# The frequency stage of a metaformer block in a new step: the spectral product is turned by VectorE in 32x32 blocks and not by way of memory

## The chip, the cores and the metric

The kernel runs on one core of a Trainium2 chip. A core has TensorE (matmuls), VectorE, ScalarE, GpSimd (POOL), SyncE (SP, which issues transfers here) and 16 DMA engines. The metric is the device time of one launch, in microseconds (us). A second source is one execution recorded by the hardware profiler.

## What is computed

Input x has 32 images of 64 channels with 56 x 56 = 3136 tokens, float32. A first half normalizes over channels, convolves with a binary 3x3 weight and adds residuals. Then the tokens t pass through a layer norm and a spectral unit, whose result is added to t. Cut to what matters here:

```python
Vf = rfft(phi, n=4096, axis=0)                    # 16 filters
Uf_p = rfft(u, n=4096, axis=1)                    # u: image, token, channel
U_plus = irfft(Vf[None, :, :, None] * Uf_p[:, :, None, :], n=4096, axis=1)[:, :sl]
out = einsum('btkd,k,kde->bte', U_plus, s, Mpp)   # and the same for U_minus, and a short AR term
```

In the kernel all filters and channel matrices are folded into one 64 x 64 complex matrix H(f) per frequency, so that the unit becomes: transform the tokens, multiply each frequency's image-by-channel matrix by H(f), transform back.

## The kernel before

There are three parts: a preparation, a first loop over 16 pairs of images (normalization, convolution, first step of the transform; writes z), the frequency stage (`mix_frequencies`, line 905), and `finish`, which makes the last step of the inverse and adds the residual. The change lies in the frequency stage alone.

The stage runs over 32 units (`NUNIT`) of 64 frequencies (`NF`). `two_by_two` writes the first two units out and loops over pairs of the others, one body for each parity (`slot`). Each engine has its own program; they meet by semaphores. For unit u:

- **p_v** (line 1058): one matmul makes the filter spectra, which VectorE copies to `v_mov` in two instructions (1150, 1153).
- **x** (1069), 4 chunks of 4 matmuls on the whole array: the forward step of the images. The copies to `xf` are four instructions a chunk.
- **h** (1078), 16 chunks of 8 float16 matmuls in two 64-column tiles: H of each frequency, saved to `hf`.
- **mix** (1090), 4 chunks of 16 matmuls in four 32-column tiles: the product. The rows of the result are images, its columns (real or imaginary, channel). It is saved to `y_sb`, stored to memory (`y_scratch`, line 964) and loaded back with frequencies as rows (`yt`, 969). This turns it.
- **inv** (1105), 16 matmuls in eight tiles of 32 rows by 64 columns: the inverse step, saved to `wf`. GpSimd stores it to `w_scratch` with eight DMAs (1020).

A chunk is one bank of PSUM: `ring` has seven banks of 512 float32 and p_v has the eighth. The order is the list `PLAN`: x 4, h 16, inv 4, mix 4, in all 28 chunks. Chunk p has bank p % 7, and is saved by ScalarE where p is even and by VectorE where it is odd. In every unit the inverse is that of unit u - 2 (`LAG_INV`), so that y has time to go out and come back. After unit 31 there are two rounds with only an inverse.

Each engine works strictly in the order of that list. TensorE waits before each chunk until the earlier chunk of the same bank is saved (`bank_free`, 1033). The inverse waits for all four of its banks at once, for `yt` and for its matrix. The first mix chunk waits until all h are saved. The saving engine waits until its chunk is ready (`chunk_ready`), and for the first inverse chunk also for `w_free`: `wf` is there once, and POOL gives it free when its stores of the unit before have landed.

SP's queue, in `body` (972): after x chunk 3 the load of z and `fwd` for unit u + 2; after the last mix copy the y store and the load of `inv`; a wait for the store; the two y loads. After unit 1 four early loads for `finish` (`load_x1`, 988; 1568 KB each) follow in the same queue.

## Time and profile before

| | us |
|---|---|
| median of three runs | 1436.41 |
| lowest, highest | 1433.49, 1443.66 |
| profiled execution, its own time | 1433.59 |
| its span | 1431.9 |
| TensorE busy | 1174.5 (82%) |
| VectorE busy | 954.0 (67%) |
| ScalarE busy | 798.9 (56%) |
| GpSimd busy | 498.9 (35%) |

The span is cut into 40 slices on the page, here of 35.8 us each. The frequency stage's steps begin at 628.69 us (slice 18) and its last copy starts at 1170.69 us; after 1182.29 `finish` has begun to load. Busy time of TensorE is pipelined and its ends are modelled, so where the length of a piece of work counts, the start of the next one is taken. PEld is the loading of weights, which overlaps. A timeline row with a count merges so many instructions; the idle time in brackets is what stood before the first, with what ended it. The profile's line 1197 is ScalarE's copy helper and 1213 VectorE's, so tile names tell the copies apart.

### The profile page before, as it was taken

Reading aid. Unit: us, or ns where it says so; the run is one execution under the profiler, and the core shown is the slowest. Engines: PE = TensorE matmul, PEld = TensorE weight load, DVE = VectorE, ACT = ScalarE, POOL = GpSimd, SP = SyncE. Lnnn points to the kernel's source line nnn. Section 1 sums busy time; section 2 is a strip of 40 time slices with the busy share of each in tenths; the row PEclk is TensorE's granted clock in tenths of the full one; section 3 lists DMA queues with packets and bytes.
Section 4 is the critical chain, followed back from the end, with each engine's and each line's share of the span. In section 5 each row is a group of like instructions: output and inputs, shape, how many; then the busy total and the mean of one; then the engine's idle time right before and its main releaser. Section 6 shows DMA issues by size and latency. Waiting matters only on the chain. (4 is left out here: it accounts for less than half of the span.)

```text
span 1431.9 us, 37537 instructions
## 1 busy us (share of the span) xinstructions
PE 1174.5 (82%) x15089; PEld 779.4 (54%) x15089; DVE 954.0 (67%) x1420; ACT 798.9 (56%) x1487; POOL 498.9 (35%) x440
## 2 busy tenths in 40 slices
PE   1899999999999977688698998999899926865667
PEld 1455555555555543147577777777777713433334
DVE  5288888888888888636477777677777713433334
ACT  1787788778887853335366666566656612322223
POOL 2146556666655567200122332232232230000000
PEclk9999999999999988669899999999999977988778
DMA  7024545554455448426899999899989969978873
GB/s 228 1 91 133 166 155 182 188 162 149 154 181 172 149 133 185 140 82 187 263 281 300 270 283 299 272 275 291 291 267 284 284 177 359 406 313 341 327 314 135
DMA packets 179624, 317.66 MB, mean 222 GB/s; under 512 B 14805, under 2 KB 154423, under 8 KB 162935
## 3 DMA queue, kind: packets, MB, share of 16 engines
q1 hardware_dynamic: 164966, 257.47, 56.6%
q0 software_dynamic: 14592, 59.26, 11.8%
q8 instruction: 47, 0.77, 0.2%
q14 instruction: 19, 0.16, 0.0%
HBM read 162.93 MB, written 153.76 MB: 221 GB/s over the span
## 5 line engine op out<-in xcount | busy, mean ns | idle before, releaser
L1020 POOL DMA_DIRECT2D w_scratch<-wf x256 | 151.2, 594 | 430.5 <-ACT y_sb L1197 391.5
L491 POOL TENSOR_TENSOR u_t<-u_t,root 98x1024 f32<-98x1024 f32 x62 | 118.0, 1935 | 169.2 <-DVE root L799 169.2
L535 PE MATMUL ring_norm<-x_all,center 128*128 128x448 f32 (+2 forms) x384 | 148.1, 511 | 24.9 <-PEq L211 15.7
L1402 ACT ACTIVATE out_sb<-p_turn 128x392 f32<-128x392 f32 x128 | 62.7, 498 | 189.6 <-PE p_turn L1358 177.7
L1346 PE MATMUL p_out<-w_in,last_masked 128*98 128x512 f32 x256 | 141.2, 636 | 23.8 <-DMA w_in<-w_scratch 23.8
L1078 PE MATMUL ring<-v_mov,m_sta 105*64 105x128 f16 x4096 | 147.2, 221 | 14.3 <-DVE xf L1213 11.6
L1213 DVE COPY hf<-ring 128x512 f32<-128x512 f32 x256 | 156.1, 682 | 1.0
L1197 ACT ACTIVATE hf<-ring 128x512 f32<-128x512 f32 x256 | 144.7, 597 | 4.9
L1391 DVE TENSOR_TENSOR x_in<-p_out,x_in 98x512 f32<-98x512 f32 x96 | 65.4, 690 | 123.1 <-DMA x_in<-x_scratch 68.3
L594 PE MATMUL ring_norm<-u_t,step_masked 98*128 98x512 f32 x256 | 126.7, 623 | 21.9 <-POOL u_t L491 21.9
L1078 PEld LDWEIGHTS ring<-v_mov,m_sta 105*64 105x64 f16 x4096 | 119.9, 110 | 40.2 <-DVE xf L1213 16.8
L1090 PE MATMUL ring<-hf,xf 128*32 128x128 f32 x4096 | 123.3, 278 | 19.1 <-ACT wf L1197 8.8
L1090 PEld LDWEIGHTS ring<-hf,xf 128*32 128x32 f32 x4096 | 113.0, 112 | 45.0 <-issue 30.6
L491 POOL TENSOR_TENSOR xc_t<-xc_t,root 98x1024 f32<-98x1024 f32 x64 | 119.7, 1900 | 50.7 <-DVE root L799 50.7
L1197 ACT ACTIVATE xf<-ring 64x256 f32<-64x256 f32 x256 | 98.5, 385 | 66.8 <-PE ring L1069 64.5
L1213 DVE COPY xf<-ring 64x256 f32<-64x256 f32 x256 | 108.2, 423 | 32.4 <-PE ring L1069 28.1
L1069 PE MATMUL ring<-fwd,z_in 128*128 128x128 f32 x1024 | 122.2, 279 | 0.0
L1069 PEld LDWEIGHTS ring<-fwd,z_in 128*128 128x128 f32 x1024 | 121.7, 196 | 0.1
L535 PEld LDWEIGHTS ring_norm<-x_all,center 128*128 128x128 f32 x384 | 66.6, 192 | 84.5 <-issue 44.9
L1358 PEld LDWEIGHTS p_turn<-ident,x_in 98*128 98x128 f32 x384 | 47.1, 153 | 120.1 <-DVE x_in L1391 67.5
L567 PE MATMUL p_conv<-signs_padded,conv_w 64*64 64x392 bf16 x2304 | 109.2, 330 | 0.2 <-DVE x_all L755 0.2
L624 ACT ACTIVATE xc_t<-ring_norm 98x512 f32<-98x512 f32 x128 | 78.7, 615 | 46.1 <-PE ring_norm L546 46.1
(132 smaller groups left out, 1923.1 us busy)
## 6 DMA issues: line engine op xcount, KB each, us to landing
z_in<-z_scratch SPq DMA_DIRECT2D x32, 1076.5 KB, 9.7
z_scratch<-z_sb SPq DMA_DIRECT2D x16, 2048.0 KB, 8.9
y_scratch<-y_sb SPq DMA_DIRECT2D x32, 1024.0 KB, 12.7
yt<-y_scratch SPq DMA_DIRECT2D x64, 512.0 KB, 6.2
w_scratch<-wf POOLq DMA_DIRECT2D x256, 128.0 KB, 7.6
w_in<-w_scratch SPq DMA_DIRECT2D x8, 4096.0 KB, 15.8
x_all<-in_x SPq DMA_DIRECT2D x16, 1568.0 KB, 7.6
x_scratch<-x_t SPq DMA_DIRECT2D x16, 1568.0 KB
```

The source lines that it names most:

```text
L491: return eng.tensor_tensor(v, v, r, ALU.mult)
L535: nc.tensor.matmul(bank_of("cen", q, c)[:, 0:WID * n], keep["center"][:, h, :], x_of(q)[:, WID * row:WID * row + WID * n], start=True, sto ...
L567: mm = nc.tensor.matmul(bank[CH * out:CH * out + CH, h, 0:CW], keep["conv_w"][CH * k:CH * k + CH, t, CH * k:CH * k + CH], pad[q % 2][CH * ...
L594: nc.tensor.matmul(bank_of("z", q, c), keep["step1"][:, c // 2, :], u_t[q % 2][:, c, :], start=True, stop=True).then_inc(z_ready, 1)
L624: nc.scalar.activation(xc_t[q % 2][:, c, :], bank, ACT.Copy).then_inc(xt_copied, 1)
L1020: nc.gpsimd.dma_start(w_units[u, h, s, c], wf[64 * c:64 * c + 64, 2 * h + s].rearrange("p (g n) -> p g n", n=256)).then_inc(w_stored, 16)
L1069: mm = nc.tensor.matmul(bank[:, 128 * j:128 * j + 128], z_in[slot][:, at:at + 2 * CH], fwd[slot][:, NF:3 * NF], start=True, stop=True)
L1078: mm = nc.tensor.matmul(bank[CH * n:CH * n + CH, 2 * NF * i:2 * NF * i + 2 * NF], m_sta[:, e, :], v_mov[:, NF * (1 - n):NF * (3 - n)], sta ...
L1090: mm = nc.tensor.matmul(bank[32 * j:32 * j + 32, 128 * i:128 * i + 128], xf[:, f, :], hf[:, f, :, :].rearrange("p r e -> p (r e)"), start= ...
L1197: return nc.scalar.activation(dst, src, ACT.Copy)
L1213: return nc.vector.tensor_copy(dst, src)
L1346: nc.tensor.matmul(p_out[0:NB, c % BANKS, :], keep["last"][:, ACH * c // MASKG, :], w_in[w_slot][:, ACH * c:ACH * c + ACH, 128 * slot:128 ...
```

## The change

A step now makes mix and inverse of unit u - 1 and x and h of unit u (`LAG` 1). The order is mix 0, x 0, mix 1, x 1, mix 2, x 2, mix 3, x 3; then four turns; then h 0 to 15; then the inverse. Banks come from a table: mix 3 to 6, x 0, 1, 2, 0, h and inverse as `BANKS` says. `xf` is there twice.

y doesn't go to memory. The four mix banks are read by VectorE with `transpose`, which turns each block of 32 x 32: rows (partitions) of a block become its columns. Four instructions (turn 0 to 3) take 16 channels each, from all four banks, 512 elements per partition, and write `yt` with channels innermost, so each instruction's elements lie 256 bytes apart in the order it writes them. The 32 columns of a block are the real and imaginary parts of 16 frequencies for one channel, its 32 rows the images; turned, frequencies are rows. The order in which mix takes the frequencies (`f`) and the rows of the constant `inv` are rearranged to match. ScalarE and VectorE don't copy y. A mix bank is free when turn 3 is done.

The inverse has 8 matmuls in four tiles of 64 x 64, one pass, with contiguous moving rows. It waits for turn 3 and for its banks 6, 1, 2 and 0.

Saving: x and inverse chunks alternate between ScalarE (even) and VectorE (odd). Of the h chunks VectorE saves 2, 5, 8, 11 and 14 and ScalarE the other eleven; before it was eight each. The y store and loads leave SP's queue, the tensor `y_scratch` goes, and after unit 31 there is one round with mix, turns and inverse.

```diff
-    inv = inv.transpose(0, 1, 4, 2, 3, 5).reshape(NUNIT, 2 * NALPHA, 128)
-    inv = np.concatenate([inv, inv], 1)
+    inv = inv.transpose(0, 1, 4, 2, 3, 5).reshape(NUNIT, 4, 16, 2, 2 * NA)
+    inv = inv.transpose(0, 1, 3, 2, 4).reshape(NUNIT, 128, 2 * NA)
...
-PLAN = [("x", 4), ("h", 16), ("inv", 4), ("mix", 4)]
-TAIL = ("inv",)
-LAG_INV = 2
+TAIL = ("mix", "turn", "inv")
+LAG = 1
 RING = 7
-
-
-def unit_chunks():
-
-    seen, out = {}, []
-    for stage, count in PLAN:
-        for _ in range(count):
-            k = seen.get(stage, 0)
-            seen[stage] = k + 1
-            out.append((stage, k, len(out)))
-    return out
+FIRST_MIX = 3
+
+H_ON_VECTOR = (2, 5, 8, 11, 14)
+
+BANKS = {"mix": (3, 4, 5, 6), "x": (0, 1, 2, 0), "h": (1, 2, 0, 1, 2, 0, 3, 4, 5, 6, 1, 2, 0, 3, 4, 5),
+         "inv": (6, 1, 2, 0)}
+
+
+def owner(stage, k):
+
+    if stage == "turn":
+        return 1
+    return int(k in H_ON_VECTOR) if stage == "h" else k % 2
+
+
+def step_chunks():
+
+    out = []
+    for k in range(4):
+        out += [("mix", k), ("x", k)]
+    out += [("turn", k) for k in range(4)]
+    out += [("h", k) for k in range(16)]
+    out += [("inv", k) for k in range(4)]
+    return [(stage, k, p) for p, (stage, k) in enumerate(out)]
...
-        inv = [sb(f"inv{i}", [128, 2, 2 * NA]) for i in range(2)]
-        xf = sb("xf", [128, NF, NIMG])
+        inv = [sb(f"inv{i}", [128, 2 * NA]) for i in range(2)]
+        xf = [sb(f"xf{i}", [128, NF, NIMG]) for i in range(2)]
         hf = sb("hf", [128, NF, 2, CH])
 
-        y_sb = [sb(f"y_sb{i}", [128, NF // 4, 2 * CH]) for i in range(2)]
-        yt = [sb(f"yt{i}", [128, NIMG // 2, 2, CH]) for i in range(2)]
+        yt = sb("yt", [128, NIMG, CH])
...
-            def store_y(slot):
-                sp.dma_start(d["y"][slot].rearrange("i p n -> p i n"), y_sb[slot][:]).then_inc(y_stored[slot], 16)
-
-            def load_y(slot):
-                for h in range(2):
-                    src = d["y"][slot].rearrange("i (j m) n -> (i j) m n", j=4)[:, 16 * h:16 * h + 16, :]
-                    sp.dma_start(yt[slot][64 * h:64 * h + 64].rearrange("p m r e -> p (m r e)"),
-                                 src.rearrange("f m n -> f (m n)")).then_inc(y_loaded[slot], 16)
+                sp.dma_start(inv[slot][:], d["c_inv"][u]).then_inc(inv_loaded[slot], 16)
 
             def body(u, slot, use):
 
+                sp.wait_ge(chunk_ready, chunks_until(u, pos["x", 3]))
+                after_wait(sp, sp_turn)
                 if not known(u, NUNIT - 2, NUNIT - 1):
-                    sp.wait_ge(chunk_ready, chunks_until(u, pos["x", 3]))
-                    after_wait(sp, sp_turn)
                     load(u + 2, slot)
-                for e in range(2):
-                    sp.wait_ge(saved[e], chunks_until(u, pos["mix", 3], e))
-                after_wait(sp, sp_turn)
-                store_y(slot)
                 if not known(u, 0, 1):
                     load_inv(u, slot)
-                sp.wait_ge(y_stored[slot], 16 * use)
-                after_wait(sp, sp_turn)
-                load_y(slot)
...
-                    pool.wait_ge(saved[e], chunks_until(u + LAG_INV, pos["inv", 3], e))
+                    pool.wait_ge(saved[e], chunks_until(u + LAG, pos["inv", 3], e))
...
+            stage, k, _ = chunks[at]
+            if stage == "mix":
+                stage, k, at = chunks[pos["turn", 3]]
+            eng.wait_ge(saved[owner(stage, k)], chunks_until(w, at, owner(stage, k)))
...
-                            all_saved(pe, u, pos["h", 15])
-                            if is_first(u):
+                            all_saved(pe, u - 1, pos["h", 15])
+                            if known(u, LAG):
                                 pe.wait_ge(reals_done, 3)
                         for i in range(4):
                             for j in range(4):
-                                f = 16 * k + 4 * i + j
-                                mm = nc.tensor.matmul(bank[32 * j:32 * j + 32, 128 * i:128 * i + 128], xf[:, f, :],
-                                                      hf[:, f, :, :].rearrange("p r e -> p (r e)"),
+                                f = 16 * j + 4 * k + i
+                                mm = nc.tensor.matmul(bank[32 * j:32 * j + 32, 128 * i:128 * i + 128],
+                                                      xf[1 - slot][:, f, :], hf[:, f, :, :].rearrange("p r e -> p (r e)"),
                                                       start=True, stop=True, tile_position=(0, 32 * j))
+                        mm.then_inc(chunk_ready, 1)
                     else:
 
                         if k:
                             continue
                         for at in range(4):
                             bank_free(pe, u, pos["inv", at])
-                        pe.wait_ge(y_loaded[slot], 32 * (use - 1))
-                        pe.wait_ge(inv_loaded[slot], 16 * (use - 1))
-                        for c in range(2):
-                            for r in range(2):
-                                for n in range(4):
-                                    rows = slice(32 * n, 32 * n + 32)
-                                    mm = nc.tensor.matmul(
-                                        ring[64 * c:64 * c + 64, pos["inv", n] % RING, :], inv[slot][rows, r, :],
-                                        yt[slot][rows, 8 * c:8 * c + 8, r, :], start=(r == 0), stop=(r == 1),
-                                        tile_position=(32 * n, 64 * c))
-                                    if c and r:
-                                        mm.then_inc(chunk_ready, 1)
-                    if stage != "inv":
-                        mm.then_inc(chunk_ready, 1)
+                        pe.wait_ge(saved[1], chunks_until(u, pos["turn", 3], 1))
+                        pe.wait_ge(inv_loaded[1 - slot], 16 * (use if slot else use - 1))
+                        after_wait(pe, pe_turn)
+                        for h in range(2):
+                            for c, row in ((0, 0), (1, 1), (1, 0), (0, 1)):
+                                images = slice(16 * h + 8 * c, 16 * h + 8 * c + 8)
+                                rows = slice(64 * row, 64 * row + 64)
+                                mm = nc.tensor.matmul(
+                                    bank_of("inv", 2 * h + row)[64 * c:64 * c + 64, :],
+                                    inv[1 - slot][rows, :], yt[rows, images, :],
+                                    start=True, stop=True, tile_position=(64 * row, 64 * c))
+                                if c != row:
+                                    mm.then_inc(chunk_ready, 1)
...
-                        eng.wait_ge(w_free, u - 1)
-                    if (stage, k) == ("mix", first_mix) and not known(u, 0, 1):
-                        eng.wait_ge(y_stored[slot], 16 * (use - 1))
...
-                    elif stage == "mix":
-                        copy(y_sb[slot][:, 4 * k:4 * k + 4, :].rearrange("p i n -> p (i n)"), bank
-                             ).then_inc(saved[which], 1)
+                    elif stage == "turn":
+                        e = slice(16 * k, 16 * k + 16)
+                        nc.vector.transpose(
+                            yt[:].rearrange("p i e -> p e i")[:, e], ring[:, FIRST_MIX:FIRST_MIX + 4, :]
+                            .rearrange("p b (i r e) -> p e r (b i)", r=2, e=CH)[:, e]).then_inc(saved[which], 1)
...
-            for u in (NUNIT, NUNIT + 1):
-                unit(u, u % 2, u // 2 + 1, False, True)
+            unit(NUNIT, NUNIT % 2, NUNIT // 2 + 1, False, True)
```

## Rows read from the trace of the kernel before

**Rows 1.** The page: busy time of the engines (us, share of the span, instructions).

```profile
PE 1174.5 (82%) x15089; PEld 779.4 (54%) x15089; DVE 954.0 (67%) x1420; ACT 798.9 (56%) x1487; POOL 498.9 (35%) x440
```

**Rows 2.** Windows, whole stage: us, busy time by engine, PEclk, DMA share, GB/s.

```profile
646.69:1134.11 487.42, 431.12 (x9632) 359.91 (x9628) 348.92 (x658) 292.59 (x598) 133.57 (x226) 0.99 0.91 276
```

**Rows 3.** Waits, 640 to 1140: who waited for whom, us, times, longest.

```profile
PE ring L1105 <- DVE hf L1213: 26.3, 29, 1.2
...
PE ring L1078 <- DVE xf L1213: 10.9, 30, 0.4
```

**Rows 4.** Timeline, one steady step: start, us, engine, line, out<-in, idle before.

```profile
899.93 3.73 PE L1069 MATMUL ring<-fwd,z_in 128*128 128x128 f32 x32
...
901.03 1.57 ACT L1197 ACTIVATE xf<-ring 64x256 f32<-64x256 f32 x4 [1.64 <-PE ring L1069]
...
901.92 3.52 DVE L1213 COPY xf<-ring 64x256 f32<-64x256 f32 x8 [0.79 <-PE ring L1069]
...
903.60 1.53 PE L1078 MATMUL ring<-v_mov,m_sta 105*64 105x128 f16 x48
904.41 4.65 ACT L1197 ACTIVATE hf<-ring 128x512 f32<-128x512 f32 x8
905.47 4.88 DVE L1213 COPY hf<-ring 128x512 f32<-128x512 f32 x8
...
905.49 3.15 PE L1078 MATMUL ring<-v_mov,m_sta 105*64 105x128 f16 x80 [0.36 <-DVE xf L1213]
...
909.58 2.01 PE L1105 MATMUL ring<-yt,inv 32*64 32x512 f32 x32 [0.93 <-DVE hf L1213]
...
911.51 3.70 PE L1090 MATMUL ring<-hf,xf 128*32 128x128 f32 x128
911.74 1.09 ACT L1197 ACTIVATE wf<-ring 128x512 f32<-128x512 f32 x2 [2.68 <-PE ring L1105]
911.80 1.29 DVE L1213 COPY wf<-ring 128x512 f32<-128x512 f32 x2 [1.45 <-PE ring L1105]
...
915.14 0.57 PE L1058 MATMUL p_v<-fwd,z_in 128*105 128x192 f32 x2
```

**Rows 5.** Timeline, the first two units of the stage.

```profile
628.69 0.97 PE L1058 MATMUL p_v<-fwd,z_in 128*105 128x192 f32 x2 [1.56 <-DVE m_sta L1242]
...
635.62 1.73 DVE L1213 COPY xf<-ring 64x256 f32<-64x256 f32 x4 [0.77 <-PE ring L1069]
...
642.36 0.19 DVE L1183 TENSOR_SCALAR hf<-hf 64x64 f32<-64x64 f32 x1
...
643.06 3.70 PE L1090 MATMUL ring<-hf,xf 128*32 128x128 f32 x128 [2.51 <-DVE hf L1187]
...
657.66 5.37 PE L1090 MATMUL ring<-hf,xf 128*32 128x128 f32 x128 [1.85 <-DVE hf L1213]
```

**Rows 6.** Timeline, the end of the stage.

```profile
1134.11 0.57 PE L1058 MATMUL p_v<-fwd,z_in 128*105 128x192 f32 x2
...
1166.84 3.69 PE L1105 MATMUL ring<-yt,inv 32*64 32x512 f32 x32 [13.12 <-DMA yt<-y_scratch]
...
1170.69 1.29 DVE L1213 COPY wf<-ring 128x512 f32<-128x512 f32 x2 [8.58 <-PE ring L1105]
```

**Rows 7.** The page: DMA issues (count, KB each, us to landing), the y store.

```profile
y_scratch<-y_sb SPq DMA_DIRECT2D x32, 1024.0 KB, 12.7
```

**Rows 8.** Groups by form, VectorE: busy us, mean ns, idle before.

```profile
L1213 DVE COPY y_sb<-ring 128x512 f32<-128x512 f32 x64 | 44.1, 691 | 56.7 <-PE ring L1090 56.7
```

**Rows 9.** Windows in the mix of unit 1: the granted clock.

```profile
658.00:660.00 2.00, 2.00 (x53) 2.00 (x48) 0.00 (x0) 0.60 (x1) 0.00 (x0) 0.59 0.95 229
```

**Rows 10.** Timeline, steps 2 and 3: early x1 load, first w store.

```profile
670.66 0.56 SPq L990 DMA_DIRECT2D x_all<-x_scratch  x1
...
677.23 5.04 POOL L1020 DMA_DIRECT2D w_scratch<-wf  x8 [81.68 <-ACT y_sb L1197]
...
708.92 1.08 ACT L1197 ACTIVATE wf<-ring 128x512 f32<-128x512 f32 x2 [14.19 <-POOLq L1024]
```

More of the change, by code:

```diff
@@ L888, in chunk_is_there @@
 def chunk_is_there(stage, u):
-    return (u >= LAG_INV) if stage in TAIL else (u < NUNIT)
+    return (u >= LAG) if stage in TAIL else (u < NUNIT)
 def chunks_until(u, p, engine=None):
-    plan = unit_chunks()
+    if engine is None:
+        mine = [(stage, at) for stage, k, at in step_chunks() if stage != "turn"]
+    else:
+        mine = [(stage, at) for stage, k, at in step_chunks() if stage != "mix" and owner(stage, k) == engine]
     if isinstance(u, int):
-        return sum(1 for w in range(u + 1) for stage, _, at in plan
-                   if chunk_is_there(stage, w) and (w < u or at <= p) and engine in (None, at % 2))
@@ L900, in chunks_until @@
-    per_unit = sum(1 for _, _, at in plan if engine in (None, at % 2))
-    missing = LAG_INV * sum(1 for stage, _, at in plan if stage in TAIL and engine in (None, at % 2))
-    return per_unit * u - missing + sum(1 for _, _, at in plan if at <= p and engine in (None, at % 2))
+        return sum(1 for w in range(u + 1) for stage, at in mine
+                   if chunk_is_there(stage, w) and (w < u or at <= p))
+    missing = LAG * sum(1 for stage, at in mine if stage in TAIL)
+    return len(mine) * u - missing + sum(1 for stage, at in mine if at <= p)
@@ L905, in mix_frequencies @@
 def mix_frequencies(nc, d, keep):
-    chunks = unit_chunks()
-    NCH = len(chunks)
-    assert NCH % RING == 0 and NCH % 2 == 0
+    chunks = step_chunks()
     pos = {(s, k): p for s, k, p in chunks}
@@ L1027, in _, with bank_of @@
             store(0)
-            with pool.Fori(1, NUNIT - LAG_INV) as u:
+            with pool.Fori(1, NUNIT - LAG) as u:
                 store(u)
-            for u in range(NUNIT - LAG_INV, NUNIT):
+            for u in range(NUNIT - LAG, NUNIT):
                 store(u)
+        def bank_of(stage, k):
+            return ring[:, BANKS[stage][k], :]
         def bank_free(eng, u, p):
+            stage, k, _ = chunks[p]
+            same = [at for other, n, at in chunks if other != "turn" and BANKS[other][n] == BANKS[stage][k]]
             if not isinstance(u, int):
-                w, at = (u, p - RING) if p >= RING else (u - 1, p - RING + NCH)
-                eng.wait_ge(saved[at % 2], chunks_until(w, at, at % 2))
-                return
-            before = [(w, at) for w in range(u + 1) for stage, _, at in chunks
-                      if chunk_is_there(stage, w) and at % RING == p % RING and (w < u or at < p)]
-            if before:
+                w, at = (u, max(at for at in same if at < p)) if min(same) < p else (u - 1, max(same))
+            else:
+                before = [(w, at) for w in range(u + 1) for at in same
+                          if chunk_is_there(chunks[at][0], w) and (w < u or at < p)]
+                if not before:
+                    return
                 w, at = before[-1]
-                eng.wait_ge(saved[at % 2], chunks_until(w, at, at % 2))
+            stage, k, _ = chunks[at]
+            if stage == "mix":
+                stage, k, at = chunks[pos["turn", 3]]
+            eng.wait_ge(saved[owner(stage, k)], chunks_until(w, at, owner(stage, k)))
         def all_saved(eng, u, p):
@@ L1060, in unit @@
                 for stage, k, p in chunks:
-                    if not (tail if stage in TAIL else head):
+                    if stage == "turn" or not (tail if stage in TAIL else head):
                         continue
@@ L1064, in unit @@
                         bank_free(pe, u, p)
-                    bank = ring[:, p % RING, :]
+                    bank = bank_of(stage, k) if stage != "inv" else None
                     if stage == "x":
@@ L1139, in saver @@
         def saver(eng, which, copy):
-            mine = [(stage, k) for stage, k, p in chunks if p % 2 == which]
+            mine = [(stage, k) for stage, k, p in chunks if stage != "mix" and owner(stage, k) == which]
             first_inv = min(k for stage, k in mine if stage == "inv")
-            first_mix = min(k for stage, k in mine if stage == "mix")
             last_h = max(k for stage, k in mine if stage == "h")
```

29 lines of the change are left out of this document (13 added, 16 removed).

## The prediction

> **What bounds the kernel now.** I read the page first (busy shares, slices, costliest groups), then the windows of the frequency stage, the timeline of one step, the waits, and last the two ends of the stage. The page has TensorE busy for most of the span [rows 1]. In the frequency stage it is busy 431 of 487 us at a mean granted clock of 0.99 [rows 2], against 349 us for VectorE and 293 for ScalarE. The DMA share of 0.91 looks like a rival bound, but among the waits of the stage none has a transfer releasing a matmul; the one case by a detour lies in its first steps [rows 10]. TensorE's regular idle spots are the inverse, which waits for the last h copies (26.3 us over 29 steps), and the seventh h chunk, whose bank waits for the last xf copy (10.9 us over 30) [rows 3]. So a steady step is a TensorE step with about 1.3 us of holes.
>
> The timeline gives its parts [rows 4]. x runs from 899.93 to 903.60, 3.67 us. Six h chunks (48 matmuls) take 1.53 us, 0.255 each where nothing holds them. After a wait, the other ten take 3.15 us, held by the copies. The inverse takes 1.93 us (909.58 to 911.51), the mix 3.63 (to 915.14), and the p_v matmul 0.41 (the rest of the 15.62 us step). Steps 0 to 31 start at 628.69 and 1134.11 [rows 5, 6], so the mean is 16.3 us. The steady one is 15.6, and the rest lies in the first steps.
>
> **What goes.** The y store and both y loads of each unit leave SP's queue: 2 MB a unit [rows 7] of some 4.3 (276 GB/s for 15.6 us). They are hidden in the steady steps, so there they are worth nothing; if that cover were gone each would cost its landing time, 12.7 us for the store. At the end they do show: unit 31's inverse starts at 1166.84 after 13.12 us of waiting for yt, and the last wf copy ends at 1170.69 + 1.29 = 1171.98 [rows 6]. Four y_sb copies a unit (about 1.28 us on VectorE, as two copies at 0.64, and as much on ScalarE) go too.
>
> **What comes, and where it stands.** VectorE gets four block turns a unit, each 512 elements per partition from PSUM, and keeps five h copies instead of eight; ScalarE gets eleven. Added up, neither becomes the bound. VectorE: v_mov 0.83, x 3.52, turns 2.6, h 5 x 0.61, inverse copies 1.29, together 11.3 us. ScalarE: 3.14 + 11 x 0.58 + 1.09 = 10.6 us. TensorE's own work is unchanged, about 14 us. The inverse has half the matmuls, but each drives twice the rows in four 64x64 tiles instead of eight 32x64 ones, so I leave it at 1.93. Judged by sums, the step should shrink.
>
> It doesn't, because of the order. VectorE works its list as written: x1, x3, four turns, then h2, h5 and so on. h2 lies in bank 0, and h5 in bank 0 too. TensorE issues in order, so h5, and all ten chunks and the inverse behind it, wait until VectorE has copied x3, made four turns and copied h2. Counted from the start of p_v:
>
> - p_v 0.41, x 3.67, mix 3.63 alternating; seven more changes between whole array and column tiles. These changes cost little in the trace (the inverse-to-mix passage is within 1.93), and I add 0.05 each: x3 ends at 8.06.
> - VectorE starts its copy 0.18 later (ScalarE's first xf copy, 901.03, against the first x chunk's end, 899.93 + 0.92) and needs 3.52 / 2 = 1.76 us [rows 4]: 10.00.
> - Four turns at 0.65: 12.60. h2's copy, 0.61: 13.21. h5 starts at 13.26.
> - h6 is ready at 13.77; ScalarE starts 0.18 later and makes five copies (h6, h7, h9, h10, h12) at 4.65 / 8 = 0.58 us: 16.85. Bank 0 holds h12 and is one of the inverse's.
> - TensorE ends h15 at 13.26 + 11 x 0.255 = 16.07, waits 0.8, and makes the inverse from 16.90 to 18.83.
>
> The next p_v stands there: a step of 18.8 us with 4.7 us of holes (1.5 before h2, 2.4 before h5, 0.8 before the inverse) against 15.6. What waits behind h5 on TensorE is the inverse, so wf, POOL's stores of w, and the next step's mix.
>
> **The turn's price.** No row shows one. The nearest are copies of 512 elements out of PSUM: 691 ns alone, 0.64 back to back for y_sb's or wf's plain order (two in 1.29), 0.61 for hf's [rows 4, 8]. Below, I bound it by an element rate without any start cost: the reduce-free slope between the 256-element xf copy (0.44 pitch) and the 512-element one (0.61) is 0.34 us per 512, so 0.34 is the floor. Above, I take twice the 0.61 of hf, 1.22, for a turn that is passed over twice. I take 0.65, since pattern and size are nearest to the copies. Each 0.1 us of a turn is 0.4 us of step and 12.4 us in all.
> The Trainium skill speaks both ways. "Vector Engine (DVE) Microarchitecture Reference", on the reshape front end, has the 32x32 turn sustain one element per cycle per lane. "Advanced Engine Details and Errata", Memory Cachelines, says that accesses that each fall on another SBUF line of 16 bytes pay a penalty. The turn writes 4 bytes every 256. By the first a turn costs about what a copy does, by the second more. No row of before writes in such steps, so it stands as a rival below.
>
> **TensorE's clock.** The mix of unit 0 took 3.70 us after 2.5 us of idling, but that of unit 1, after 1.85 us, took 5.37 [rows 5], at a clock of 0.59 from 658 to 660 [rows 9]. So a hole of the size that each new step has can cost 1.67 us, or nothing. I put that at one step in five, 0.3 us: 19.1 us a step. The Trainium skill's "TensorE: Matmul & The Clock Gate", on PSUM-queue cycling, tells of the same: short idles between groups of matmuls make the clock go up and down.
>
> **The ends of the stage.** Step 0 has no mix and no turns. ScalarE gets h0 and h1, waits for h2 (its bank needs the x3 copy, 637.35), then makes nine copies, to about 643.2; three small fixes of the first unit (0.70, as before) bring the first mix to 643.9, against 643.06 [rows 5]. There are then 31 steps to the mix of unit 31, which comes 0.4 earlier for want of a p_v: 643.9 + 31 x 19.1 - 0.4 = 1235.6. After it: mix 3.63, turns 0.16 + 2.6, inverse 1.98, copies 0.85, in all 9.2: 1244.8. Last, the early x1 loads: issued at 670.66, before the first store of w (677.23), they held the next wf copies until 708.92 [rows 10]. Now they are issued near 652 and should be through near 686, where the second unit's wf copy is due at 680.5: 6 us. The last wf copy ends at 1250.8, 78.8 later than before's 1171.98. What follows (POOL's stores, 12 us to the first w) is the same. Against the profiled execution's own 1433.59 us (span 1431.9, 1.7 around it): 1512. That execution is 3 us under the median of the three runs, within their spread.
>
> **Rivals.**
> *The clock falls in most steps* (0.17). For it: the hole before h5 follows another of 1.5 us with only 0.77 us of work between. Against: steady steps keep 1.00 with holes of 0.9. Then +1.7 a step instead of 0.3: 1512 + 31 x 1.4 = 1555, more if the inverse too is at half speed.
> *The turn costs twice a copy* (0.18): the Trainium skill's penalty, here 1.22 instead of 0.65, four times on the path: +2.3 a step, 1583.
> *Faster* (0.05): the one thing that decides is whether h5 waits behind the turns. If VectorE had h2 saved by the time TensorE asks, the step would be 8.06 + 16 x 0.255 + 0.8 + 1.93 = 14.9 and the kernel would end at 643.9 + 461.9 - 0.4 + 9.2 = 1114.6, 57 before now: 1376. The bound lies at a step of (1171.98 - 643.9 + 0.4 - 9.2 - 6) / 31 = 16.6, which needs turns of about 0.1 us. The list order speaks against it.
> *Near equal* (0.05, of which 0.03 within 1%): turns near the floor, 0.34, with cheap changes give 17.2 to 17.5 a step, still over 1%; only with a shorter h stage as well does it reach 1440.
>
> **Numbers.** My case (step 18.2 to 19.8) has 0.55 and gives 1478 to 1534, likeliest 1512. The range takes in the clock rival whole and most of the dear turn: 1475 to 1585. A per cent either way is what a measurement can tell. Faster 0.05, same 0.03, slower 0.92.
>
> **What would show it.** In the steady steps of the new profile: starts of p_v 18.5 to 19.5 us apart; before h2 and h5 TensorE idle about 1.5 and 2.4 us, released by VectorE; turns of 0.65 to 0.7 us standing between VectorE's x3 and h2 copies; ScalarE idle near 1.9 us before h6; DMA share down by nearly half with no gain. Wrong would be: turns of over 1 us, granted clocks under 0.95 in the stage, x and mix together longer than 7.7 us, or h5 released by anything but VectorE.

## The result, and the profile after

The changed kernel takes 1597.9 us (median of four runs, 1594.74 to 1598.76) against 1434.95 for the kernel before (four runs on the same chip): a ratio of 1.112, 95% interval 1.108 to 1.116. Slower was forecast, and by the mechanism forecast, but the time lies above the range (1475 to 1585). The profiled execution took 1598.08 us.

The page of the changed kernel, busy time of the engines (as [rows 1]):

```profile
PE 1260.8 (79%) x14577; PEld 830.8 (52%) x14577; DVE 980.6 (61%) x1388; ACT 813.4 (51%) x1519; POOL 498.9 (31%) x440
```

TensorE executes 512 matmuls fewer than before and is busy 86 us longer. The groups on the page (line, engine, operation, out<-in, count | busy, mean ns | idle before, releaser) show 48 us of it in h. This is the row of h in the kernel before:

```profile
L1078 PE MATMUL ring<-v_mov,m_sta 105*64 105x128 f16 x4096 | 147.2, 221 | 14.3 <-DVE xf L1213 11.6
```

And these are the rows of h and of the turns in the changed kernel; the price of a turn is far over that of the copy in [rows 8]:

```profile
L1081 PE MATMUL ring<-v_mov,m_sta 105*64 105x128 f16 x4096 | 195.1, 276 | 145.5 <-DVE hf L1214 105.5
...
L1176 DVE STREAM_TRANSPOSE yt<-ring 128x512 f32<-128x512 f32 x128 | 118.3, 1045 | 3.9 <-PE ring L1094 2.9
```

The waits of the changed kernel from 640 to 1300 us (as [rows 3]: who waited for whom, us, times, longest):

```profile
PE ring L1081 <- DVE hf L1214: 102.1, 31, 3.4
...
PE ring L1081 <- DVE xf L1214: 37.7, 30, 1.3
```

The first is h5's wait for its bank, the second h2's. These idle times of TensorE are called holes below. A steady step in the timeline of the changed kernel (as [rows 4]: start, us, engine, line, out<-in, idle before):

```profile
907.82 0.57 PE L1060 MATMUL p_v<-fwd,z_in 128*105 128x192 f32 x2
...
908.33 1.08 PE L1094 MATMUL ring<-hf,xf 128*32 128x128 f32 x32
...
909.34 1.16 PE L1071 MATMUL ring<-fwd,z_in 128*128 128x128 f32 x8
...
910.42 1.08 PE L1094 MATMUL ring<-hf,xf 128*32 128x128 f32 x32
...
916.72 0.64 PE L1081 MATMUL ring<-v_mov,m_sta 105*64 105x128 f16 x16
916.83 1.73 DVE L1214 COPY xf<-ring 64x256 f32<-64x256 f32 x4 [2.47 <-PE ring L1071]
...
918.59 3.70 DVE L1176 STREAM_TRANSPOSE yt<-ring 128x512 f32<-128x512 f32 x4
...
918.62 0.86 PE L1081 MATMUL ring<-v_mov,m_sta 105*64 105x128 f16 x24 [1.26 <-DVE xf L1214]
...
922.13 0.68 DVE L1214 COPY hf<-ring 128x512 f32<-128x512 f32 x1
...
922.87 4.90 PE L1081 MATMUL ring<-v_mov,m_sta 105*64 105x128 f16 x88 [3.39 <-DVE hf L1214]
```

The inverse follows at 927.70 and the next p_v at 930.37. The step is x3's copy, four turns, h2's copy, and only then h5, with TensorE idle beside it. The same step in windows (us, busy by engine, PEclk, DMA share, GB/s), cut at h0, at h5 and at the inverse:

```profile
907.82:916.72 8.90, 8.90 (x166) 7.38 (x162) 3.12 (x7) 3.67 (x9) 4.72 (x8) 1.00 0.44 118
916.72:922.87 6.15, 1.50 (x41) 1.18 (x41) 5.91 (x9) 2.17 (x4) 0.00 (x0) 0.97 0.60 201
922.87:927.70 4.83, 4.83 (x88) 4.66 (x88) 2.38 (x4) 3.25 (x6) 0.00 (x0) 0.50 0.00 0
927.70:930.36 2.66, 2.66 (x18) 0.70 (x16) 1.06 (x2) 1.19 (x2) 0.00 (x0) 0.69 0.00 0
```

The third line is the surprise: when TensorE resumes after the hole, its granted clock is 0.50, the lower of its two levels (1.2 GHz), for all of h5 to h15. It fell in the last 0.4 us of the hole (the 0.97 of the second line). That comes back in every steady step, where the mean from h5 to the inverse is 0.50 to 0.64, 0.55 on average. From 700 to 1100 us the mean granted clock is 0.86, against 0.99 over the stage before [rows 2].

The end of the stage in the changed kernel (as [rows 6]):

```profile
1322.90 3.70 PE L1094 MATMUL ring<-hf,xf 128*32 128x128 f32 x128
...
1326.67 3.60 DVE L1176 STREAM_TRANSPOSE yt<-ring 128x512 f32<-128x512 f32 x4 [2.90 <-PE ring L1094]
...
1330.67 3.69 PE L1111 MATMUL ring<-yt,inv 64*64 64x512 f32 x16 [4.07 <-DVE yt L1176]
...
1334.45 0.69 DVE L1214 COPY wf<-ring 128x512 f32<-128x512 f32 x1 [1.02 <-PE ring L1111]
```

The steps are 21.78 us long on average from the fifth on (21.3 to 22.6); before, that mean was 15.65. Below, "the step" is this mean. Average parts of it, again from the fifth step on: h5 starts 15.05 us after p_v, the inverse 4.63 later, and the next p_v 2.10 after that.

### The profile page after: what moved, and what is told of

The parts are those of the page before. It is cut to its first block and busy times, and to the rows that moved or that the text cites. A ratio compares the mean times of both kernels' runs of the same rounds, so it can differ in the third digit from the quotient of the medians.

```text
span 1596.4 us, 36484 instructions
## 1 busy us (share of the span) xinstructions
PE 1260.8 (79%) x14577; PEld 830.8 (52%) x14577; DVE 980.6 (61%) x1388; ACT 813.4 (51%) x1519; POOL 498.9 (31%) x440
## 5 line engine op out<-in xcount | busy, mean ns | idle before, releaser
L1081 PE MATMUL ring<-v_mov,m_sta 105*64 105x128 f16 x4096 | 195.1, 276 | 145.5 <-DVE hf L1214 105.5
L1199 ACT ACTIVATE hf<-ring 128x512 f32<-128x512 f32 x352 | 190.9, 596 | 185.5 <-PE ring L1081 184.8
L1081 PEld LDWEIGHTS ring<-v_mov,m_sta 105*64 105x64 f16 x4096 | 178.4, 149 | 159.8 <-DVE hf L1214 110.6
L1214 DVE COPY hf<-ring 128x512 f32<-128x512 f32 x160 | 109.8, 687 | 74.4 <-PE ring L1081 74.0
L1071 PE MATMUL ring<-fwd,z_in 128*128 128x128 f32 x1024 | 150.6, 292 | 0.5 <-DVE wf L1214 0.5
L1071 PEld LDWEIGHTS ring<-fwd,z_in 128*128 128x128 f32 x1024 | 127.0, 195 | 25.3 <-issue 24.2
L1094 PE MATMUL ring<-hf,xf 128*32 128x128 f32 x4096 | 138.5, 277 | 1.8 <-DVE hf L1189 1.8
L1176 DVE STREAM_TRANSPOSE yt<-ring 128x512 f32<-128x512 f32 x128 | 118.3, 1045 | 3.9 <-PE ring L1094 2.9
L1094 PEld LDWEIGHTS ring<-hf,xf 128*32 128x32 f32 x4096 | 104.8, 110 | 21.6 <-issue 7.5
```

What stands on the lines that cost most here:

```text
L1071: mm = nc.tensor.matmul(bank[:, 128 * j:128 * j + 128], z_in[slot][:, at:at + 2 * CH], fwd[slot][:, NF:3 * NF], start=True, stop=True)
L1081: mm = nc.tensor.matmul(bank[CH * n:CH * n + CH, 2 * NF * i:2 * NF * i + 2 * NF], m_sta[:, e, :], v_mov[:, NF * (1 - n):NF * (3 - n)], sta ...
L1094: mm = nc.tensor.matmul(bank[32 * j:32 * j + 32, 128 * i:128 * i + 128], xf[1 - slot][:, f, :], hf[:, f, :, :].rearrange("p r e -> p (r e) ...
L1176: nc.vector.transpose(yt[:].rearrange("p i e -> p e i")[:, e], ring[:, FIRST_MIX:FIRST_MIX + 4, :] .rearrange("p b (i r e) -> p e r (b i)" ...
L1199: return nc.scalar.activation(dst, src, ACT.Copy)
L1214: return nc.vector.tensor_copy(dst, src)
```

## The experiments

"Ratio" is to the kernel before on the same chip. Edits are to the changed kernel unless a diff says otherwise.

### The order on VectorE: three ways to shorten the wait before h5

**1. All mix ahead of x.** It takes away six of the seven changes between column tiles and the whole array, and moves nothing between engines.

```diff
-    for k in range(4):
-        out += [("mix", k), ("x", k)]
+    out += [("mix", k) for k in range(4)]
+    out += [("x", k) for k in range(4)]
```

> The changed kernel with one edit: TensorE makes mix 0 to 3 and then x 0 to 3, instead of taking them in turn; everything else, VectorE's order (x1, x3, turns, h2) among it, stays. In the changed kernel mix and x together take 8.39 us where before took 3.67 + 3.63 = 7.30. If the changes between whole array and column tiles cost this (7 more a step), the step shrinks by 0.8 to 1.0 us, 31 steps give 25 to 31 us: about 1570. If the passage between the two is free and the 8.39 has another cause (waits on banks, the loads of weights), mix and x stay at 8.4 and the time at 1598.

Measured: 1557.76 us, ratio 1.086 [1.082, 1.089], step 20.52. Its timeline, mix, x and h0:

```profile
916.02 3.70 PE L1094 MATMUL ring<-hf,xf 128*32 128x128 f32 x128
919.65 3.99 PE L1071 MATMUL ring<-fwd,z_in 128*128 128x128 f32 x32
923.60 0.41 PE L1081 MATMUL ring<-v_mov,m_sta 105*64 105x128 f16 x8
```

From 916.02 to 923.60 is 7.58 us, where the changed kernel needs 8.39 (908.33 to 916.72). Six changes fewer give back 0.81 us, 0.14 each. The step is 1.26 us shorter, more than was expected, and the time lies below 1570. The hole before h2 is shorter (0.79 instead of 1.26), but h1 now waits 0.24, so that h5 starts only 0.86 earlier. The other 0.4 us come behind it: from h5 to the inverse 4.46 us instead of 4.63, and 1.88 to p_v instead of 2.10. The hole before h5 stays, 3.38 us: it isn't the alternation that makes it.

**2. The turns ahead of x** (as above, with the turns between mix and x).

> As the last one, and the four turns stand before x in every list, so VectorE turns while TensorE makes x, and then copies x1 and x3 before h2. Theory (the order on VectorE is what costs): the turns, 3.7 us, no longer stand between x3 and h5. What is left of the wait is the two x copies (3.5 us) after the turns: step about 18 to 18.5 us instead of 21.6 to 22.5, time 1480 to 1500. Rival (the sum of work on VectorE or the price of the turns as such counts): VectorE has the same work per step, so the step stays within 1 us of that of mix first, time 1540 to 1570.

Measured: 1505.87 us, ratio 1.049 [1.045, 1.054], step 18.80. The turns run beside x, and h5 waits at most 0.34 us instead of 3.39; VectorE's x copies are late now, so h0 waits 1.60 and h2 1.05. The step lies a little above the 18 to 18.5 expected. In the fourth step the stall of the early x1 loads is back (27.1 us). Against the first experiment, from which it differs in the place of the turns alone, the step is 1.72 us shorter with all work kept: that place is a cause. If the summed work of VectorE set the step, it could not have helped.

**3. h2 saved by ScalarE**, which waits for no turn.

```diff
-H_ON_VECTOR = (2, 5, 8, 11, 14)
+H_ON_VECTOR = (5, 8, 11, 14)
```

> The changed kernel with h2 saved by ScalarE and not by VectorE. Bank 0 is then free for h5 before the turns are done, and only h6 has to wait, for turn 3 itself. Theory (h5 waits for h2 behind the turns): the long wait moves from h5 to h6 and is over when turn 3 ends, one copy (0.65 us) earlier, with one chunk less left to make: step 0.7 to 1.1 us shorter, time 1565 to 1577. Rival (h5's wait is for the turns' banks anyway and h2 has no part in it): nothing, 1595 to 1600; ScalarE, with one copy more, would make it slower by at most 0.5 us a step.

Measured: 1557.27 us, ratio 1.086 [1.083, 1.089], step 20.47. Its timeline:

```profile
903.71 0.41 PE L1081 MATMUL ring<-v_mov,m_sta 105*64 105x128 f16 x8 [0.25 <-ACT hf L1199]
...
906.33 3.87 PE L1081 MATMUL ring<-v_mov,m_sta 105*64 105x128 f16 x80 [2.21 <-DVE yt L1176]
```

h5 goes early, and h6, which needs mix's first bank, now waits for the last turn by name. One copy off the chain is worth 1.3 us a step, about twice its length of 0.68 and more than was expected: the wait ends a copy earlier, there is a chunk less to make behind it, and the mean clock from 700 to 1100 us is 0.89 instead of 0.86. How the 1.3 us divide among the three was not measured.

### TensorE's clock: fill the holes

**4. 128 more float16 matmuls a step**, four groups of eight behind h2's place and twelve behind h5's, into an unused part of p_v's bank.

```diff
+FILL = {2: 4, 5: 12}
...
+                    if stage == "h" and tail:
+                        for _ in range(FILL.get(k, 0)):
+                            for i in range(4):
+                                for n in range(2):
+                                    nc.tensor.matmul(p_v[CH * n:CH * n + CH, 384:512], m_sta[:, i, :],
+                                                     v_mov[:, NF * (1 - n):NF * (3 - n)], start=True, stop=True,
+                                                     tile_position=(0, CH * n))
```

> The changed kernel with more work: in both holes before h2 and before h5 TensorE makes 4 and 12 further chunks of h matmuls (8 each, into an unused part of the p_v bank), results unused. Theory (the half clock after the holes costs): TensorE has 4.1 us more to do a step and is still faster, since the clock stays at 1.0: h5 to h15 with the wait behind them take about 3.5 us instead of 4.8 and the inverse 1.93 instead of up to 2.7; with up to 0.3 us lost where the filling runs over, a step 1.2 to 1.9 us shorter, 1540 to 1562. Rival (the chunks are slow because the copies hold them, not because of the clock): no shorter step, and with the filling 1598 to 1610.

Measured: 1656.59 us, ratio 1.154 [1.151, 1.158], step 23.95. Slower, not faster, and both theories missed. Its timeline, and its queue of instruction packets on the page (packets, MB, share):

```profile
906.25 0.57 PE L1061 MATMUL p_v<-fwd,z_in 128*105 128x192 f32 x2 [2.13 <-issue]
...
909.45 1.22 PE L1102 MATMUL ring<-hf,xf 128*32 128x128 f32 x17 [2.06 <-issue]
...
925.89 2.65 PE L1089 MATMUL ring<-v_mov,m_sta 105*64 105x128 f16 x88 [0.81 <-DVE hf L1222]
...
929.37 1.95 PE L1119 MATMUL ring<-yt,inv 64*64 64x512 f32 x16 [0.83 <-ACT hf L1207]
```

```profile
q8 instruction: 176, 2.88, 0.7%
```

From h5 to the inverse it takes 3.48 us instead of 4.63 on average: where the holes are filled (0.36 and 0.81 us are left of them), the clock holds. But in every second step TensorE stands still twice for some 2 us with nothing that the profile names. Counted from inverse to inverse, the steps alternate between 20.5 and about 27.2 us: a step without such stops is already 1.3 us shorter than the changed kernel's. The instruction packets go from 47 (0.77 MB) to 176 (2.88 MB). That these stops are the fetching of a longer loop body fits both numbers, but it was only argued; the next run tests the filling with few instructions.

**5. Eight long matmuls a step** (float32, 320 columns) in the same places.

```diff
+FILL = {2: 2, 5: 6}
...
+                    if stage == "h" and tail:
+                        for _ in range(FILL.get(k, 0)):
+                            nc.tensor.matmul(p_v[:, 192:512], keep["center"][:, 0, :],
+                                             keep["last"][:].rearrange("p g b -> p (g b)")[:, 0:320],
+                                             start=True, stop=True)
```

> The holes before h2 and h5 are filled again, now with 2 and 6 long float32 matmuls (whole array, 320 columns, into the unused part of the p_v bank, results unused), 8 more matmuls a step and not 128. In the run with 128 the packets of instruction loads rose from 47 to 176 and TensorE had idle spots of 2.1 us before p_v and in the first mix chunk that nothing in the profile ends, while between h5 and the inverse its steps were 3.5 us as forecast. Theory (two things were mixed: the clock's cost of about 1.9 us a step, and a body of too many instructions that is fetched anew): the packets stay at 47, the idle spots are gone, the clock stays at 1.0, and a step is 19.8 to 20.3 us, time 1540 to 1556. Rival (the filling itself disturbs): again over 1598.

Measured: 1564.45 us, ratio 1.089 [1.083, 1.094], step 20.47. It adds work to TensorE and takes 33 us off the kernel. Instruction packets are 47 again and no stop without a name is left. Its windows from 700 to 1100, and its step:

```profile
700.00:1100.00 400.00, 382.74 (x6277) 283.26 (x6279) 246.14 (x412) 195.45 (x411) 89.66 (x152) 1.00 0.37 112
```

```profile
907.98 3.50 PE L1068 MATMUL p_v<-last_masked,center 128*128 128x320 f32 x12
911.50 2.65 PE L1087 MATMUL ring<-v_mov,m_sta 105*64 105x128 f16 x88
...
914.97 1.95 PE L1117 MATMUL ring<-yt,inv 64*64 64x512 f32 x16 [0.83 <-ACT hf L1205]
...
916.85 0.57 PE L1061 MATMUL p_v<-fwd,z_in 128*105 128x192 f32 x2
```

h5 starts 15.12 us after its step's p_v (896.38), as in the changed kernel (15.05). Everything that was gained lies behind it: 3.47 us to the inverse and 1.88 to p_v, in place of 4.63 and 2.10 on average. So the low clock costs 21.78 - 20.47 = 1.31 us a step. The forecast was a step shorter still (19.8 to 20.3); the time also has the early stall again, 6 us in its fourth step.

### What makes the turn dear

A turn took 1045 ns, against 0.65 us in the sum. Three theories: the turning itself; the writes of 4 bytes every 256; the reads in steps of 512 bytes from four banks.

**6. A plain copy with the turn's two patterns** (`tensor_copy` in place of `transpose`; blocks aren't turned).

> Each turn of the changed kernel is an ordinary copy with the same reads from PSUM (every 512 bytes) and the same writes (4 bytes every 256); the blocks are not turned, so the result is another. It tells whether the 0.92 us of a turn (3.70 for four) come from the operation or from where it writes. Theory A (the writes in wide steps cost): it stays at 0.85 to 0.95 and the time at 1590 to 1600. Theory B (the operation costs): it falls to 0.61 to 0.69, four turns are 1.0 to 1.2 us shorter, and the time is 1555 to 1568.

**7. A turn that writes end to end** and reads as before.

```diff
-                            yt[:].rearrange("p i e -> p e i")[:, e], ring[:, FIRST_MIX:FIRST_MIX + 4, :]
+                            yt[:].rearrange("p i e -> p (i e)")[:, 512 * k:512 * k + 512]
+                            .rearrange("p (e i) -> p e i", i=NIMG), ring[:, FIRST_MIX:FIRST_MIX + 4, :]
```

> The turn stays a block turn with the same reads, but writes its 512 elements one after another (the result is another). Theory A (the writes in wide steps cost): four turns fall from 3.70 us to 2.5 to 2.8. Theory B (the operation costs): 3.6 to 3.75 as before. Time by A about 1560, by B about 1597.

**8. A turn that reads one bank end to end** and writes as before.

> The turn stays, and writes as in the changed kernel, but reads one bank from end to end and not every 512 bytes over four banks (the result is another). If the reads are a part of the price (theory C), four turns fall from 3.70 us to under 3.4; by theories A and B they stay at 3.6 to 3.75, time 1597.

The groups of VectorE into yt, in this order (busy us, mean ns):

```profile
L1176 DVE COPY yt<-ring 128x512 f32<-128x512 f32 x128 | 117.3, 1037 | 3.9 <-PE ring L1094 2.9
```

```profile
L1176 DVE STREAM_TRANSPOSE yt<-ring 128x512 f32<-128x512 f32 x128 | 80.3, 685 | 3.9 <-PE ring L1094 2.9
```

```profile
L1176 DVE STREAM_TRANSPOSE yt<-ring 128x512 f32<-128x512 f32 x128 | 118.3, 1042 | 3.9 <-PE ring L1094 2.9
```

Steps were 21.68, 20.42 and 21.80 us, times 1594.2 (ratio 1.108 [1.103, 1.114]), 1555.07 and 1595.96 (one run each). The copy is as dear as the turn, so turning costs nothing. Plain reads save nothing. Plain writes bring the turn to the 691 ns of [rows 8]. It is the writes alone: 1045 / 685 = 1.53. With the cheap turn of the seventh experiment the hole before h5 is 2.26 us, and the clock falls all the same. Its h5 to h15, and its windows from 700 to 1100:

```profile
904.87 4.90 PE L1081 MATMUL ring<-v_mov,m_sta 105*64 105x128 f16 x88 [2.26 <-DVE hf L1215]
```

```profile
700.00:1100.00 400.00, 331.15 (x5994) 262.27 (x5995) 222.49 (x411) 200.84 (x414) 91.98 (x156) 0.87 0.37 111
```

**9. Images innermost in yt**, so that the turn writes end to end and its reader takes the steps: the inverse reads runs of eight images (32 bytes), and the wf copies put the order right.

```diff
-                            yt[:].rearrange("p i e -> p e i")[:, e], ring[:, FIRST_MIX:FIRST_MIX + 4, :]
+                            yt[:, e, :], ring[:, FIRST_MIX:FIRST_MIX + 4, :]
...
-                                    inv[1 - slot][rows, :], yt[rows, images, :],
+                                    inv[1 - slot][rows, :], yt[rows, :, images],
...
-                        copy(wf[:, k, :], bank).then_inc(saved[which], 1)
+                        copy(wf[:, k, :].rearrange("p (i e) -> p i e", e=CH),
+                             bank.rearrange("p (e i) -> p i e", e=CH)).then_inc(saved[which], 1)
```

> The changed kernel with yt laid out with images innermost: a turn writes its 512 elements one after another; the inverse then reads runs of 8 elements in 64 places, and the copies to wf put the order right by reading PSUM in steps. The result is the reference's. Theory (the writes in wide steps cost 0.3 us a turn, reads in steps cost nothing): turns 2.5 us for four, inverse 1.95 us, wf copies 0.6 and 0.69 as before, a step 20.3 to 20.5, time 1553 to 1562. Rival (the price only moves to the readers): the inverse takes over 2.5 us or the copies over 0.8, and the time is 1580 or more.

Expected was 1553 to 1562 us if the price goes, and 1580 or more if it only moves to the readers. Measured: 1561.14 us, ratio 1.087 [1.083, 1.091], step 20.51. Turns take 685 ns, wf copies 692 on VectorE and 597 on ScalarE (as the changed kernel's), and a matmul of the inverse 666 ns on average against 680. The price was lifted, not moved. The new layout, made so that the inverse reads in plain order, is thus paid by the writer and gives the reader nothing.

### A better order

**10. The order, banks and owners chosen anew**, turns as they are: TensorE gets x1 to x3 and the first h chunks to do while VectorE turns.

```diff
+ORDER = ("x0 mix0 mix1 mix2 mix3 turn0 h0 h1 h2 turn1 turn2 h3 turn3 h4 x1 h5 h6 h7 h8 h9 x2 h10 h11 "
+         "h12 h13 x3 h14 h15 ")
+ON_VECTOR = (('h', 7), ('h', 10), ('h', 11), ('h', 12), ('h', 15), ('inv', 1), ('x', 1))
+BANKS = {"mix": (3, 4, 5, 6), "x": (0, 1, 5, 2),
+         "h": (2, 0, 1, 2, 0, 2, 0, 4, 2, 6, 1, 0, 6, 3, 4, 0),
+         "inv": (5, 1, 3, 6)}
```

> The changed kernel's work and layout, channels innermost and turns of 0.92 us, in another order, with another table of banks and owners: x 0, mix 0 to 3, then the h chunks and x 1 to 3 mixed in among the turns, so that TensorE always has a chunk whose bank is free. Theory (nothing but the order and its holes makes the step long; no engine has more than 14 us of work): a step of 15.2 to 15.8 us at a clock near 1.0, and with the ends as in the changed kernel, 1385 to 1415, below the kernel before. Rival (the turns' price or VectorE's sum of work counts): step not under 18, time over 1480.

Measured: 1419.28 us, ratio 0.989 [0.986, 0.992], step 15.66, clock 1.00. With turns of 1026 ns still in it, the step is that of before (15.65). So another order, with its banks and owners, takes back all 6.1 us a step that were lost. The last wf copy ends 16.5 us before that of the kernel before: 6.4 lie in the first four steps and 10.1 behind the start of the last one, where nothing waits for yt from memory any more. Whether the kernel before would itself gain from a new order was not tried, so this is no measure of what dropping y's way through memory is worth in a step. The time lies just above what was forecast (1385 to 1415).

**11. Both**: cheap turns and an order made for them.

```diff
+ORDER = ("mix0 mix1 mix2 mix3 turn0 h0 turn1 h1 turn2 x0 turn3 h2 x1 h3 h4 h5 h6 x2 h7 h8 h9 h10 h11 "
+         "h12 h13 h14 h15 x3 ")
+ON_VECTOR = (('h', 2), ('h', 3), ('h', 4), ('h', 5), ('h', 9), ('h', 10), ('h', 13), ('h', 14),
+             ('inv', 0), ('inv', 3), ('x', 2))
+BANKS = {"mix": (3, 4, 5, 6), "x": (2, 1, 2, 0),
+         "h": (1, 0, 0, 6, 4, 5, 0, 6, 3, 1, 4, 0, 6, 3, 5, 2),
+         "inv": (2, 4, 1, 6)}
```

> A new order as in the last one (its own table, made for turns of 0.61) together with images innermost. Theory: a step of 14.2 to 14.9 us, set by TensorE's own work, and 1355 to 1385. If the last one comes out as expected and this one doesn't gain on it, the turns' price is off the path once the order is right.

Measured: 1396.95 us, ratio 0.972 [0.969, 0.976], step 14.93, at the upper end of the 14.2 to 14.9 expected. Layout and order both differ from the tenth experiment; how the 0.73 us a step divide between them was not tried. The time misses the forecast (1355 to 1385), and the timeline shows where:

```profile
686.06 1.09 ACT L1203 ACTIVATE wf<-ring 128x512 f32<-128x512 f32 x2 [10.57 <-POOLq L1020]
...
686.71 5.35 PE L1097 MATMUL ring<-hf,xf 128*32 128x128 f32 x96 [9.20 <-ACT wf L1203]
```

The second unit's wf copies wait for the first store of w, which shares the DMA engines with the four early x1 loads; mix waits behind them and then runs at the low clock (0.50). Its third and fourth steps take 18.98 and 27.07 us.

**12. One x1 load after each of steps 2 to 5** instead of four in a row.

```diff
-            for n in range(len(PREFETCHED)):
-                load_x1(n)
-            with sp.Fori(1, NUNIT // 2 - 1) as h:
+            for u in range(2, 2 + len(PREFETCHED)):
+                body(u, u % 2, u // 2 + 1)
+                load_x1(u - 2)
+            with sp.Fori(3, NUNIT // 2 - 1) as h:
```

> The new order with images innermost and one more edit: the four early x1 loads (1568 KB each) are not issued together after unit 1 but one after each of the units 2 to 5. In the run without it steps 2 and 3 take 19.0 and 27.1 us instead of 14.93, and TensorE waits 9.2 us for the wf copy, which waits for a store of w that shares the DMA engines with 6.3 MB of x1. Theory (that collision costs 4.1 + 12.2 us): both steps fall to 15 to 16.5 us, time lower by 10 to 16 us, 1381 to 1388. Rival (the first store of w is slow for another reason, as when GpSimd starts its queue): the steps stay and the time is 1395 to 1399.

Measured: 1383.49 us, ratio 0.963 [0.960, 0.966], within the forecast of 1381 to 1388. The steps are so only in part: the third and fourth, 18.98 and 27.07 before this edit, should both have come to 15 to 16.5. The first steps are 13.74, 16.04, 15.74 and 19.25, all others 14.93. So the loads in a row are a cause of the stall, and 4.3 us remain in the fourth step. Windows of this kernel from 700 to 1100:

```profile
700.00:1100.00 400.00, 393.22 (x8202) 318.12 (x8204) 299.57 (x537) 271.12 (x591) 124.38 (x211) 1.00 0.51 160
```

TensorE is busy 393 of 400 us. Its last wf copy ends at 1121.99, 50.0 before that of the kernel before (1171.98 [rows 6]): 27 steps give 19.3 us, the first four 18.1, and the end of the stage, without the wait for yt and without a second round, 12.6.

## Why the prediction was right in kind and wrong in size

**Right: where h5 waits, and for whom.** h2 and h5 are released by VectorE in 30 and 31 cases, with idle times of 1.3 and 3.4 us (forecast 1.5 and 2.4). The second and third experiments showed it as a cause: turns moved, or h2 moved, and the wait shrinks. The rivals "faster" and "near equal" are out; DMA fell from [rows 2]'s 0.91 to 0.36 (640 to 1300 us) with no gain in a steady step, as said. Three of the prediction's own signs of being wrong came: turns of over 1 us, a clock under 0.95 in the stage, and x and mix longer together than 7.7 us (8.39).

**Wrong: the turn at 0.65.** From the first turn to h2's copy it is 922.13 - 918.59 = 3.54 us, not 2.60: +0.94 a step. The step that failed was "pattern and size are nearest to the copies". Size was; the pattern of the writes was not, as the sum's own next sentences on the Trainium skill had noted. The measured price is neither rival's: by the row of the copy 0.65, by the doubled turn 1.22, measured 0.89 in a row and 1.04 alone. By "Advanced Engine Details and Errata", Memory Cachelines (the Trainium skill), each access on another line costs more; the runs agree and give it a size.

**Wrong: the changes of tiling at 0.05.** p_v to h0 took 8.90, not 8.06: +0.84. Against the 7.71 that p_v, x and mix took before it is 1.19, for which the sum had 7 x 0.05 = 0.35; the first experiment gave back 0.81 of it with six of the changes. The passage from inverse to mix, by which I judged them cheap, goes from one tiled form to another; none between tiles and the whole array had been priced. The Trainium skill has in "TensorEngine Tiling (Array Packing)", Key Properties, that a change of tiling mode drains TensorE; the trace agrees with a price for each change, here 0.14 us.

With the held clock of the fifth experiment, a step is 20.47: 18.8 + 0.94 + 0.84 and -0.1 for small terms. That part of the sum holds together.

**Wrong: the clock at 0.3 a step.** It fell in every step, after the hole, and cost 1.31. The evidence was on the table [rows 5, 9]: a hole of 1.85 us was followed by a slow mix. I took it as one case in five because another hole (2.5 us) cost nothing. The new step has two holes, 1.3 and 3.4 us, with 0.86 us of work between, which the rival had named. The dear turn isn't needed for it: with cheap turns (seventh and ninth experiments) the second hole is 2.26 us, less than the forecast's 2.4, and the mean clock from 700 to 1100 us is 0.87 and 0.85, no better than the changed kernel's 0.86. In the second experiment, with holes of 1.6, 1.05 and at most 0.34 us, it is still 0.90. Filling both kept the clock at 1.00, so the holes are the cause; whether the second alone would do it was not tried.

**The ends.** The first mix began at 644.86 (forecast 643.9). After the last mix it took 12.24 us, not 9.2: 4.00 from the first turn to the inverse instead of 2.6, and the inverse 3.69 at the low clock instead of 1.98. The early stall of 6 us did not come. The second unit's wf copies were held until 690.13, later than the 686 of the prediction; counted as [rows 10] has it (670.66 to 708.92), loads issued near 652 do give 690. But in the slower steps they had waited only 1.8 us by then, and no more than 1.0 us of it can show (the fourth step is 22.8 us). In the second, fifth and ninth to eleventh experiments, whose copies waited 4 to 11 us, the fourth step takes 25 to 27 us. The length of the steps alone does not decide it: the sixth, with a step of 21.68, has 26.15 there, and the first, third and seventh, with steps of 20.4 to 20.5, have 21.0 to 22.8.

**Together.** The last wf copy ended at 1335.14, forecast 1250.8: 84.3 later. The 31 steps from first to last mix took 678.0 instead of 591.7, +86.3, of which 31 x 1.67 = 51.8 are the two prices with the small terms, 31 x 1.01 = 31.3 the clock, and the remaining 3.2 that the first steps were longer than the mean; then +3.0 at the end, +1.0 at the start, -6.0 for the stall. Two rivals, each given under one in five, had both come partly true, and the range was made as if only one could. Its inner case has a slip as well: by the prediction's own sum a step of 18.2 gives 1484, not 1478.

## What to carry to other kernels

When in-order work is handed to another engine, count what stands behind it in that engine's list before adding up busy times: here another order, with its banks and owners, and the turns as dear as before brought 1597.9 us down to 1419.3. A hole in TensorE's work was priced twice here, as idle time and as the lower clock of what follows, so a new hole in every step calls for both prices. Rivals that don't exclude each other must be able to come true together, and the range has to hold their sum. And when a layout is chosen for its reader, price the writer: here the reader didn't care and the writer paid half as much again.

## What the runs showed of the hardware that was not expected

- VectorE writing float32 elements 256 bytes apart needs 1.04 us per 512 elements of a partition, end to end 0.685, the same for a turn and for a copy. VectorE's reads of PSUM in steps of 512 bytes cost nothing, nor do moving rows of TensorE in runs of 32 bytes (at clock 1.00 a matmul of the inverse takes 600 to 608 ns with them, 605 to 614 without).
- The turn itself, 32 x 32 blocks of float32, costs no more than a copy (685 against 691 ns).
- With holes of 1.3 and 3.4 us the granted clock over the 4.4 to 4.8 us behind them was 0.50 to 0.64 in every steady step; eight long matmuls in the holes kept it at 1.00 and saved more than they cost.
- Changing between whole-array matmuls and those in four 32-column tiles (float32) costs 0.14 us each time.
- 128 more short matmuls in the loop body of each unit made the instruction packets 176 instead of 47 and came with two idle times of about 2.1 us that no wait explains, in every second step; the cause was only argued.
- An inverse in four tiles of 64 x 64 takes 1.95 us for what eight tiles of 32 x 64 did in 2.01 [rows 4].
